# Latent attention: two float16 value parts in place of three bfloat16, and the next batch's norm steps issued earlier

## The chip, the cores and the metric

The kernel runs on one core of a Trainium2 chip. The metric is device time in microseconds, the median of several runs. Within a core TensorE (PE; its weight loads are PEld), VectorE (DVE), ScalarE (ACT) and GpSimd (POOL) each work through their own list of instructions; SyncE (SP) issues DMAs. They meet only at semaphores.

## The reference

A two-layer decoder: causal attention, cross attention and a quantized feed-forward, then an attention with a convolution over its scores, a latent attention and a mixture of experts. The change touches the latent attention alone (`ctx_1024` are 77 context rows per batch, `x` 1024 latent rows per batch; 4 batches, 4 heads of 64):

```python
xn = layernorm(x, ln_x_g, ln_x_b)            # here x is ctx_1024
ln = layernorm(latents, ln_l_g, ln_l_b)      # here the residual stream
q = ln @ W_q
kv = jnp.concatenate([xn @ W_kv, ln @ W_kv], axis=1)
k, v = (kv[..., :INNER], kv[..., INNER:])
q, k, v = (to_heads(q), to_heads(k), to_heads(v))
qn = rmsnorm(q, q_gamma) * SCALE
kn = rmsnorm(k, k_gamma)
sim = jnp.einsum('bhid,bhjd->bhij', qn, kn)
sim = jnp.where(full_mask[:, None, None, :], sim, neg)
attn = jax.nn.softmax(sim.astype(jnp.float32), axis=-1)
out = jnp.einsum('bhij,bhjd->bhid', attn, v)
return out @ W_out + b_out
```

Each query row sees 1024 own keys and 77 context keys.

## The kernel before

`stage_latent_attention` first makes keys and values of the context rows for all batches (the first block), then runs a second block over four batches. A batch has a **preparation** of 14 steps: the normalized rows are transposed, multiplied to queries, keys and values (`multiply_qk`, `multiply_v`), and queries and keys are scaled to unit size. Then comes a **loop of 32 units**. A unit is one head and one tile of 128 query rows; two units make a **pair**, 16 pairs a batch.

The way of a unit: `scores` on TensorE (query halves against the key parts `KH` and `KL`, 1102 columns), then on VectorE `maximum` (mask add, maximum, negation), on ScalarE `exps` and `high` (the float16 upper half), on GpSimd `low` (the float16 lower half, L2936), and from SP one DMA transpose (L2788), which turns both halves. When both units of a pair are turned, `mix_values` multiplies them with the values, ScalarE's `copy_mix` brings the sum to SBUF, `project` multiplies with the output weights, and VectorE's `add` adds to the residual.

The order is written by hand: each engine's block lists its steps for unit u, and `behind(b, u)` those of earlier pairs. On TensorE the mix of pair p comes in unit 2p+5, behind its scores, and the projection in unit 2p+7. The last two mixes of a batch fall into steps 1 and 3 of the next preparation. Score banks come in two, probabilities and halves in three, transposed halves and mix copies in two per pair.

Values are held in three bfloat16 parts of 64 columns: ScalarE copies the product (`value_high`), VectorE subtracts (`value_left`), ScalarE copies the rest (`value_middle`), GpSimd subtracts again (`values_low`). `mix_values` multiplies parts one and two together (128 columns wide, L2864 and L2866), and part three by itself (64 wide, L2870 and L2873, the two probability halves in different column halves of the array).

The next batch's norm runs within the loop: `stats` and `aggregate` on VectorE in units 8 to 14, seven small steps on GpSimd in units 15 to 21 (`rstd_step`; two of them are powers, L2949 and L2959), `apply` on VectorE in units 22 to 29 (L3140), and GpSimd's `add_bias` (L2932) in units 23 to 30.

## Time and profile before

| what | value |
|---|---|
| median of 3 runs | 3918.76 us (3916.62 to 3923.54) |
| profiled execution | 3912.23 us, span 3910.5 us |
| PE, share of the span | 86% |
| DVE | 75% |
| ACT | 67% |
| POOL | 47% |
| DMA queue q1, share of 16 engines | 60.7% |

The shares are means over stages with different limits. The latent attention runs from about 2678 to 3361 us of the span, so a change in it is read from rows of that stretch. A row of the timeline gives start, duration, engine, line, operation, what it writes and reads, and in brackets the idle time of the engine before it and what ended that.

### The profile page before, as it was taken

How to read it: one execution, taken by the hardware profiler on the slowest of the kernel's cores; microseconds unless marked ns; L12 is line 12 of the kernel's file. 1: busy time of each engine (PE TensorE's matmuls, PEld its weight loads, DVE VectorE, ACT ScalarE, POOL GpSimd, SP SyncE). 2: the span in 40 equal slices, each digit the busy share in tenths (PEclk: the TensorE clock that was granted, in tenths of full speed). 3: DMA queues.
4: the chain of work that ended last, by engine and by line, in shares of the span. 5: the costliest groups of instructions: out<-in, count | busy, mean ns of one | idle time of the engine just before them, and what ended most of it. 6: DMA issues, size and time to landing. Idle time of an engine off the chain costs nothing. (4 is left out here: it accounts for less than half of the span.)

```text
span 3910.5 us, 61085 instructions
## 1 busy us (share of the span) xinstructions
PE 3369.3 (86%) x20113; PEld 2602.9 (67%) x20113; DVE 2928.5 (75%) x5833; ACT 2601.1 (67%) x3897; POOL 1826.9 (47%) x1129
## 2 busy tenths in 40 slices
PE   6867724269999999999999999995889899799999
PEld 4645521147777777777777777773667667699999
DVE  4568789779888888888888889984676666474347
ACT  2334444558888888898888989982667667354443
POOL 0034410016656566565665656642767576360015
PEclk9989956589999999999999999997999999799999
DMA  1047800038889888888888889891749467743224
GB/s 51 0 87 129 147 22 1 1 110 157 151 147 154 147 151 151 146 156 143 154 146 151 155 149 162 162 165 36 124 85 174 80 121 140 204 149 95 76 83 146
DMA packets 1571351, 470.02 MB, mean 120 GB/s; under 512 B 1507174, under 2 KB 1565159, under 8 KB 1569767
## 3 DMA queue, kind: packets, MB, share of 16 engines
q1 hardware_dynamic: 1564903, 449.40, 60.7%
q0 software_dynamic: 6144, 16.79, 1.3%
q8 instruction: 164, 2.69, 0.3%
q14 instruction: 140, 1.15, 0.1%
HBM read 49.00 MB, written 39.58 MB: 23 GB/s over the span
## 5 line engine op out<-in xcount | busy, mean ns | idle before, releaser
L2331 DVE TENSOR_REDUCE d_neg_max<-psum 128x1 f32<-128x1024 f32 x512 | 624.6, 1220 | 161.9 <-PE psum L2066 160.7
L2066 PE MATMUL psum<-d_KH,d_QH 128*128 128x512 f32 x2048 | 685.3, 416 | 25.5 <-DVE d_halves L2340 21.0
L2222 ACT ACTIVATE psum<-psum,d_bias 128x1024 f32<-128x1024 f32 x512 | 558.2, 1090 | 213.9 <-DVE d_bias L2335 203.5
L2340 DVE SCALAR_TENSOR_TENSOR d_halves<-psum,d_halves 128x1024 f16<-128x1024 f32 x512 | 624.3, 1219 | 32.3 <-ACT d_halves L2229 27.7
L2066 PE MATMUL psum<-d_KL,d_QH 128*128 128x512 f32 x2048 | 638.1, 393 | 0.0
L2066 PE MATMUL psum<-d_KH,d_QL 128*128 128x512 f32 x2048 | 636.7, 392 | 0.0
L2022 POOL TENSOR_TENSOR d_KC<-d_KC,d_tap_of 128x1024 f32<-128x1024 f32 x126 | 302.1, 2397 | 536.6 <-ACT d_tap_of L2211 536.6
L2229 ACT ACTIVATE d_halves<-psum 128x1024 f16<-128x1024 f32 x512 | 521.6, 1019 | 3.5
L2066 PEld LDWEIGHTS psum<-d_KH,d_QH 128*128 128x128 f32 x2048 | 356.9, 188 | 173.1 <-issue 68.4
L2066 PEld LDWEIGHTS psum<-d_KL,d_QH 128*128 128x128 f32 x2048 | 384.9, 188 | 87.7
L2066 PEld LDWEIGHTS psum<-d_KH,d_QL 128*128 128x128 f32 x2048 | 384.9, 188 | 87.0
L2029 POOL TENSOR_TENSOR d_KL<-d_KC,d_KH 128x1024 fp32r<-128x1024 f32 x128 | 308.1, 2407 | 112.7 <-ACT d_KH L2217 112.7
L2936 POOL TENSOR_TENSOR e_halves<-e_probs,e_halves 128x1102 f16<-128x1102 f32 x128 | 292.2, 2283 | 122.9 <-ACT e_halves L3037 121.5
L2018 POOL TENSOR_TENSOR d_KC<-d_KC,d_tap_of 128x1024 f32<-128x1024 f32 x126 | 306.8, 2435 | 26.2 <-ACT d_tap_of L2211 17.9
L2211 ACT ACTIVATE d_tap_of<-d_K,d_taps 128x1024 f32<-128x1024 f32 x252 | 288.8, 1146 | 0.0
L3030 ACT ACTIVATE e_probs<-psum,e_neg_max 128x1102 f32<-128x1102 f32 x128 | 150.3, 1174 | 92.9 <-DVE e_neg_max L3109 92.8
L3105 DVE TENSOR_REDUCE e_own_neg_max<-psum 128x1 f32<-128x1102 f32 x128 | 167.1, 1305 | 4.4
L3494 POOL DMA_INDIRECT f_tile<-f_expert_out,f_slots x64 | 60.8, 950 | 231.7 <-DMA f_expert_out<-f_tile 183.8
L3781 DVE TENSOR_TENSOR f_hT_low<-psum,f_hT_high 128x384 fp32r<-128x384 f32 x135 | 75.3, 558 | 117.4 <-ACT f_hT_high L3657 117.2
L3653 ACT ACTIVATE f_silu<-psum 128x352 f32<-128x352 f32 x135 | 62.8, 466 | 145.7 <-PE psum L3543 143.0
L3037 ACT ACTIVATE e_halves<-e_probs 128x1102 f16<-128x1102 f32 x128 | 143.7, 1122 | 23.6 <-DMA e_probsT<-e_halves 20.4
L3657 ACT ACTIVATE f_hT_high<-psum 128x384 fp32r<-128x384 f32 x135 | 66.4, 492 | 137.1 <-PE psum L3563 137.0
(526 smaller groups left out, 7577.7 us busy)
## 6 DMA issues: line engine op xcount, KB each, us to landing
f_weights_raw<-in_L_ffn_packed_dram SPq DMA_DIRECT2D x10, 1088.0 KB, 16.1
f_tile<-expert_rows SPq DMA_DIRECT2D x71, 128.0 KB, 2.2
f_expert_out<-f_tile SPq DMA_DIRECT2D x71, 128.0 KB, 1.7
d_probsT<-d_halves SPq DMA_TRANSPOSE x512, 4.3
f_tile<-f_kept_rows SPq DMA_DIRECT2D x64, 128.0 KB, 2.2
expert_rows<-d_group_mixT SPq DMA_DIRECT2D x7, 1024.0 KB, 11.5
residual_stream<-in_x_dram SPq DMA_DIRECT2D x4, 1024.0 KB, 9.5
f_kept_rows<-residual_stream SPq DMA_DIRECT2D x4, 1024.0 KB, 8.5
```

The costliest lines, as they stand in the source:

```text
L2018: g.tensor_tensor(KC[:, ch, :], KC[:, ch, :], tap_of[:, ch, :], ALU.add)\
L2022: g.tensor_tensor(KC[:, ch, :], KC[:, ch, :], tap_of[:, ch, :], ALU.add)\
L2029: g.tensor_tensor(KL[hh % 2][:, ch, :], KC[:, ch, :], KH[hh % 2][:, ch, :].bitcast(F32), ALU.subtract).then_inc(key_low.sem, 1)
L2066: last = t.matmul(scores_at(u)[:, cols], q_part[:, ch, j * P:(j + 1) * P], k_part[hh % 2][:, ch, cols], start=k == 0, stop=k == 5)
L2211: a.activation(tap_of[:, ch, :], K[b % 2][:, ch, k:S + k], ACT.Copy, scale=taps[:, ch, 3 * h + k:3 * h + k + 1]).then_inc(tapped.sem, 1)
L2222: a.activation(scores_at(u), scores_at(u), ACT.Exp, bias=bias[u % 2][:, 0:1], accum_out=sums[u // 4 % 4][:, u % 4, :]).then_inc(probs_read ...
L2229: a.activation(halves[u % 4][:, 0, :], scores_at(u), ACT.Copy, scale=LIFT)\
L2331: v.tensor_reduce(neg_max[u % 2][:], scores_at(u), AXIS.X, ALU.max, negate=True)\
L2340: v.scalar_tensor_tensor(halves[u % 4][:, 1, :], scores_at(u), LIFT, halves[u % 4][:, 0, :], ALU.mult, ALU.subtract).then_inc(probs_low.se ...
L2936: g.tensor_tensor(halves[i % 3][:, 1, 0:W], probs[i % 3][:], halves[i % 3][:, 0, 0:W], ALU.subtract)\
L3030: a.activation(probs[g % 3][:], scores_at(g), ACT.Exp, bias=neg_max[g % 2][:, 0:1], accum_out=sums[p % 2][:, i:i + 1]).then_inc(probs_read ...
L3105: v.tensor_reduce(own_neg_max[g % 2][:], scores_at(u), AXIS.X, ALU.max, negate=True)\
```

## The change

Values: two float16 parts in place of three bfloat16. So that float16 can hold them, they are multiplied by a power of two, `v_scale`, which bounds them by the norm of the gains, shifts and value weights; it is worked out before the loops by three squares with sums on ScalarE, a product with ones on TensorE, a power on GpSimd and some operations of one column on VectorE. The output weights `wo` are multiplied by the inverse once, on ScalarE in unit 3 of the first batch. `value_middle`, `values_low` and the products of the third part are gone; `value_low` on VectorE multiplies and subtracts in one operation.

Norm steps: `stats` and `aggregate` start in unit 3 in place of 8, `rstd_step` in 9 in place of 15, `add_bias` in 22 in place of 23; `apply` stays in units 22 to 29. `apply` becomes a scalar_tensor_tensor with the reciprocal spread over 256 columns as second tensor.

```diff
@@ mix_values (TensorE)
-                    if p == 0:
-                        t.wait_ge(v_low.sem, v_low.at(TB * (b + 1)))
...
                     for k in range(TB):
                         for part in range(2):
-                            t.matmul(mix_bank, V[:, k, h, 0:2 * HD], moving(part, k), start=k + part == 0, stop=False)
+                            t.matmul(mix_bank, V[:, k, h, :], moving(part, k), start=k + part == 0, stop=False)
                     for part in range(2):
-                        t.matmul(mix_bank, ctx_values[:, b, h, 0:2 * HD], moving(part, TB)[0:Z, :], start=False,
-                                 stop=False)
-                    for k in range(TB):
-                        for part in range(2):
-                            t.matmul(mix_bank[part * HD:(part + 1) * HD, :], V[:, k, h, 2 * HD:3 * HD],
-                                     moving(part, k), start=False, stop=False)
-                    for part in range(2):
-                        last = t.matmul(mix_bank[part * HD:(part + 1) * HD, :], ctx_values[:, b, h, 2 * HD:3 * HD],
-                                        moving(part, TB)[0:Z, :], start=False, stop=True)
+                        last = t.matmul(mix_bank, ctx_values[:, b, h, :], moving(part, TB)[0:Z, :], start=False,
+                                        stop=part == 1)
@@ before the loops (VectorE, GpSimd, TensorE, ScalarE)
+                    v.tensor_scalar(v_size[:, 0:1], PS[:, 6 * BANK:6 * BANK + 1], float(2 * D), None, ALU.mult)
...
+                    g.wait_ge(v_scaled.sem, v_scaled.at(3))
+                    g.tensor_tensor(v_size[:, 1:2], v_size[:, 0:1], core.minus_half[:, 0:1], ALU.pow)\
+                        .then_inc(v_scaled.sem, 1)
                     norm_pool(g, n, 0, True)
...
+                    t.matmul(PS[:, 6 * BANK:6 * BANK + 3], core.ones[:], v_squares[:], start=True, stop=True)\
+                        .then_inc(v_totalled.sem, 1)
...
+                    a.activation(n.xT[:, 1, 0:DC * D], wv[:].rearrange("p c n -> p (c n)"), ACT.Square,
+                                 accum_out=v_squares[:, 2:3]).then_inc(v_squares_done.sem, 1)
@@ values (ScalarE, VectorE)
-                def value_middle(b, j):
-                    a.wait_ge(v_left.sem, v_left.at(TB * b + j + 1))
-                    a.activation(V[:, j, :, HD:2 * HD], left[j % 2][:], ACT.Copy).then_inc(v_middle.sem, 1)
...
+                def value_low(b, j):
                     v.wait_ge(v_high.sem, v_high.at(TB * b + j + 1))
-                    v.wait_ge(v_low.sem, v_low.at(TB * b + j - 1))
-                    v.tensor_tensor(left[j % 2][:], bank(j % 2)[:, 0:D].rearrange("p (h e) -> p h e", h=H),
-                                    V[:, j, :, 0:HD], ALU.subtract).then_inc(v_left.sem, 1)
+                    v.scalar_tensor_tensor(V[:, j, :, HD:2 * HD],
+                                           bank(j % 2)[:, 0:D].rearrange("p (h e) -> p h e", h=H), v_scale[:, 0:1],
+                                           V[:, j, :, 0:HD], ALU.mult, ALU.subtract).then_inc(v_low.sem, 1)
@@ units (ScalarE)
+                        if b == 0 and u == 3:
+                            a.activation(wo[:], wo[:], ACT.Copy, scale=wo_scale[:, 0:1]).then_inc(wo_scaled.sem, 1)
@@ norm steps (GpSimd, VectorE)
-                        if b + 1 < B and 15 <= u < 22:
-                            rstd_step(b + 1, u - 15)
-                        if b + 1 < B and 23 <= u < 23 + TB:
-                            add_bias(TB * (b + 1) + u - 23)
+                        if b + 1 < B and 9 <= u < 16:
+                            rstd_step(b + 1, u - 9)
+                        if b + 1 < B and 22 <= u < 22 + TB:
+                            add_bias(TB * (b + 1) + u - 22)
...
-                    v.tensor_scalar(n.xn[:, tile, :], X[:, TB * b + tile, :], n.mv[:, tile, 0:1],
-                                    n.rstd[:, tile:tile + 1], ALU.subtract, ALU.mult).then_inc(n.normed.sem, 1)
+                    v.scalar_tensor_tensor(n.xn[:, tile, :], X[:, TB * b + tile, :], n.mv[:, tile, 0:1],
+                                           n.rstd[:, tile:tile + 1].to_broadcast([P, D]), ALU.subtract, ALU.mult)\
+                        .then_inc(n.normed.sem, 1)
...
-                        if b + 1 < B and 8 <= u < 12:
-                            stats(b + 1, 2 * u - 16)
-                            stats(b + 1, 2 * u - 15)
+                        if b + 1 < B and 3 <= u < 7:
+                            stats(b + 1, 2 * u - 6)
+                            stats(b + 1, 2 * u - 5)
```

TensorE, an odd unit of the first batch's loop, in the kernel before: the projection of one pair, the mix of another, then the next unit's first scores.

```order
L2882 MATMUL psum<-e_wo,e_mixT 128x256 x2
L2864 MATMUL psum<-e_probsT,e_V 128x256 x16
L2866 MATMUL psum<-e_probsT,e_ctx_values 128x256 x2
L2870 MATMUL psum<-e_probsT,e_V 64x256 x16
L2873 MATMUL psum<-e_probsT,e_ctx_values 64x256 x2
L2845 MATMUL psum<-e_KH,e_QS 128x512
```

The same place now:

```order
L2917 MATMUL psum<-e_wo,e_mixT 128x256 x2
L2905 MATMUL psum<-e_probsT,e_V 128x256 x16
L2907 MATMUL psum<-e_probsT,e_ctx_values 128x256 x2
L2888 MATMUL psum<-e_KH,e_QS 128x512
L2889 MATMUL psum<-e_KL,e_QS 128x512
```

The 18 products of 64 columns are gone, and nothing else of the row has moved.

GpSimd, the end of the norm steps in the first batch's loop, in the kernel before (`e_ln_rstd` is the reciprocal that `apply` reads, the `residual_stream` rows are bias adds):

```order
673 L2959 TENSOR_TENSOR e_ln_tmp<-e_ln_tmp,minus_half 128x8
674 L2936 TENSOR_TENSOR e_halves<-e_probs_33320,e_halves 128x1102
675 L2962 TENSOR_TENSOR e_ln_rstd<-e_ln_tmp 128x8
676 L2936 TENSOR_TENSOR e_halves<-e_probs_33321,e_halves 128x1102
677 L2936 TENSOR_TENSOR e_halves<-e_probs_33322,e_halves 128x1102
678 L2932 TENSOR_TENSOR residual_stream<-residual_stream,e_bo 128x256
```

The same steps now:

```order
667 L2989 TENSOR_TENSOR e_ln_tmp<-e_ln_tmp,minus_half 128x8
668 L2966 TENSOR_TENSOR e_halves<-e_probs_33341,e_halves 128x1102
669 L2992 TENSOR_TENSOR e_ln_rstd<-e_ln_tmp 128x8
670 L2966 TENSOR_TENSOR e_halves<-e_probs_33342,e_halves 128x1102
671 L2966 TENSOR_TENSOR e_halves<-e_probs_33343,e_halves 128x1102
672 L2966 TENSOR_TENSOR e_halves<-e_probs_33341,e_halves 128x1102
673 L2966 TENSOR_TENSOR e_halves<-e_probs_33342,e_halves 128x1102
674 L2966 TENSOR_TENSOR e_halves<-e_probs_33343,e_halves 128x1102
675 L2966 TENSOR_TENSOR e_halves<-e_probs_33341,e_halves 128x1102
676 L2966 TENSOR_TENSOR e_halves<-e_probs_33342,e_halves 128x1102
677 L2962 TENSOR_TENSOR residual_stream<-residual_stream,e_bo 128x256
```

Between the reciprocal and the first bias add stand seven subtractions of a unit where there were two; the order of the steps is the same.

## Rows read from the trace of the kernel before

**Rows 1.** Busy by stretch: us, PE, PEld, DVE, ACT, POOL, PEclk, DMA share, GB/s.
```profile
2757.00:2867.00 110.00, 101.05 (x748) 80.86 (x747) 76.89 (x162) 78.85 (x110) 80.45 (x47) 0.94 0.92 160
...
2875.00:2906.00 31.00, 26.82 (x150) 16.62 (x147) 22.05 (x32) 16.46 (x30) 19.01 (x15) 1.00 0.00 1
...
3089.00:3098.00 9.00, 7.19 (x29) 5.31 (x28) 4.19 (x9) 6.76 (x10) 6.84 (x4) 0.52 1.12 209
```

**Rows 2.** Timeline, TensorE, one mix of the last batch and the scores behind it.
```profile
3281.15 1.91 PE L2864 MATMUL psum<-e_probsT,e_V 128*128 128x256 f16 x16
...
3283.21 1.06 PE L2870 MATMUL psum<-e_probsT,e_V 128*64 128x256 f16 x16
...
3284.32 0.50 PE L2845 MATMUL psum<-e_KH,e_QS 128*128 128x512 f32 x1
```

**Rows 3.** Timeline, TensorE, second and fourteenth mix of the second and last batch.
```profile
2940.81 1.91 PE L2864 MATMUL psum<-e_probsT,e_V 128*128 128x256 f16 x16
...
3021.78 1.91 PE L2864 MATMUL psum<-e_probsT,e_V 128*128 128x256 f16 x16
...
3261.85 1.91 PE L2864 MATMUL psum<-e_probsT,e_V 128*128 128x256 f16 x16
...
3341.21 1.91 PE L2864 MATMUL psum<-e_probsT,e_V 128*128 128x256 f16 x16
```

**Rows 4.** Timeline, the way of one pair in the last batch.
```profile
3277.89 0.50 PE L2845 MATMUL psum<-e_KH,e_QS 128*128 128x512 f32 x1
...
3281.05 0.23 DVE L3102 TENSOR_TENSOR psum<-psum,e_lowered 128x78 f32<-128x78 f32 x1
3281.08 1.18 ACT L3030 ACTIVATE e_probs<-psum,e_neg_max 128x1102 f32<-128x1102 f32 x1 [1.43 <-DVE e_neg_max L3109]
...
3282.38 1.12 ACT L3037 ACTIVATE e_halves<-e_probs 128x1102 f16<-128x1102 f32 x1
...
3283.41 1.16 ACT L3030 ACTIVATE e_probs<-psum,e_neg_max 128x1102 f32<-128x1102 f32 x1
3283.58 2.29 POOL L2936 TENSOR_TENSOR e_halves<-e_probs,e_halves 128x1102 f16<-128x1102 f32 x1 [1.84 <-ACT e_halves L3037]
...
3286.03 1.12 ACT L3037 ACTIVATE e_halves<-e_probs 128x1102 f16<-128x1102 f32 x1 [1.36 <-DMA e_probsT<-e_halves]
```

**Rows 5.** The transposes over the stage: issue on SP in ns, landing.
```profile
L2788 SPq DMA_TRANSPOSE e_probsT<-e_halves x128: 2636/2768/3834, 2764.8 to 3348.7; - x128
...
DMA to landing us min/median/max: 4.5/4.8/6.8
```

**Rows 6.** By line, ns min/median/max: apply, unit, floor; reciprocal waited for; powers.
```profile
L3140 DVE TENSOR_SCALAR e_ln_xn<-residual_stream,e_ln_mean_var,e_ln_rstd x24: 406/946/2032, 2836.8 to 3180.8; 128x256 f32<-128x256 f32 x24
...
  POOL e_ln_rstd L2962: 4.9, 3
...
L3074 DVE TENSOR_TENSOR e_unit<-e_raw,e_inv x32: 1214/1218/1745, 2722.1 to 3228.2; 128x1024 f32<-128x1024 f32 x32
...
L2918 POOL TENSOR_SCALAR e_floor<-e_size x32: 251/1152/1286, 2720.0 to 3225.0; 128x8 f32<-128x8 f32 x32
...
L2949 POOL TENSOR_TENSOR e_ln_tmp<-e_ln_tmp,minus_half 128x8 f32<-128x8 f32 x3 | 4.9, 1640 | 0.0
```

**Rows 7.** Timeline, the second batch's preparation, behind mix 14.
```profile
2876.40 3.70 PE L2808 MATMUL psum<-e_wqk,e_ln_xT 128*128 128x512 f32 x8
...
2878.43 0.60 ACT L2994 ACTIVATE e_raw<-psum 128x512 f32<-128x512 f32 x1 [4.53 <-PE psum L2808]
```

**Rows 8.** Timeline, the end of the second batch's preparation.
```profile
2911.85 0.72 ACT L3017 ACTIVATE e_V<-e_v_left 128x256 bf16<-128x256 f32 x2
...
2913.75 0.42 DVE L3096 TENSOR_TENSOR e_v_left<-psum,e_V 128x256 f32<-128x256 f32 x1 [0.20 <-POOL e_V L2927]
```

**Rows 9.** Timeline, before the loops.
```profile
2683.79 1.01 POOL L2677 TENSOR_TENSOR e_pre_rstd<-e_pre_var_eps,minus_half 77x4 f32<-77x4 f32 x1
...
2698.82 1.06 ACT L2723 ACTIVATE e_ctx_values<-e_pre_left 77x1024 bf16<-77x1024 f32 x1 [1.44 <-DVE e_pre_raw L2641]
```

115 lines of the change are left out of this document (70 added, 45 removed).

## The prediction

> **What bounds the kernel now.** I read the views in this order: the busy time by stretch, to find what stops in the stage that the change touches; the timeline of one pair of units, to see which engine sets the pace; the rows of the transposing DMA; then the waits around the norm steps. The stage runs four times through a loop of 32 units (16 pairs), with a preparation of some 50 us between two loops. In a loop TensorE is busy 101.05 of 110.00 us, and the DMA engines show a share of 0.92 [rows 1]: two candidates. The timeline says which one it is. In the last batch the scores of one pair start at 3277.89 and those of the next at 3284.32 [rows 2, 4]: 6.43 us, and TensorE works through them without a gap. So a quiet pair is bound by TensorE at 6.44. Over twelve pairs (second mix to fourteenth) the second batch takes 3021.78 - 2940.81 = 80.97 and the last, which has no norm steps, 3341.21 - 3261.85 = 79.36 [rows 3], or 6.75 and 6.61 per pair. What is over 6.44 comes from late transposes and from the norm steps.
>
> **Part 1, the third product is gone.** The 64-wide products of the third value part and their two context products run from 3283.21 to 3284.32 [rows 2]: 1.11 us per pair, so TensorE alone would go at 6.43 - 1.11 = 5.32. Full gain would be 64 x 1.11 = 71 us. It isn't reached, because another loop is next late. Mix(p) stands behind the scores of unit 2p+5 and waits for both transposes of its pair. Counted from the start of the pair's first scores (3277.89): the second unit's mask add starts at 3.16, its exponential at 5.52 [rows 4]. ScalarE's conversion follows an exponential by 3282.38 - 3281.08 = 1.30, GpSimd's subtraction that by 3283.58 - 3282.38 = 1.20 [rows 4], and it takes 2.28. That puts the second transpose at 10.3. The first unit's subtraction ends at 7.97, so its transpose holds the SP queue to 8.05 + 2.77 = 10.8 [rows 5], and the second lands at 10.9 + 4.7 = 15.6 (4.7 lies between the least and the median landing). On TensorE the mix's place comes two periods after the pair's own scores, plus the scores and the projection ahead of it, 3281.15 - 3277.89 = 3.26 [rows 2, 4]. With TensorE idle for the difference: 2C + 3.26 + (C - 5.32) = 15.6, so C = 5.9. Today 2 x 6.44 + 3.26 = 16.1 leaves 0.6 of slack, which is why a quiet pair doesn't wait.
>
> Late transposes come on top: landing takes 4.5 to 6.8 us, 4.8 in the median [rows 5], and one late by 1.4 stops ScalarE for 1.36 [rows 4]. Today they cost 6.61 - 6.44 = 0.17 per pair against a slack of 0.6. Without slack I take twice that, less for neighbours that have slack of their own: 0.3. So C = 6.2 without norm steps. Bounds: 5.66 (two SP issues of 2.77 and their gaps, no late landing) and 6.6 (each late landing counts fully and the pace stays what it is).
>
> **Part 2, norm steps.** bn_stats, bn_aggr and GpSimd's seven steps move from units 8 to 21 to units 3 to 15. Of these only the two powers of 1.64 matter on GpSimd [rows 6], which has 2.28 of work per unit of 3.1; they are only moved, and now meet a loop without slack: 0.05 per pair, 6.25. What goes is VectorE's wait for the reciprocal at unit 22: 4.9 us in three times [rows 6]. It now has six units of lead; the loop takes a part of that as its gain, already in 6.25. GpSimd's bias adds move one unit up, behind apply operations that VectorE issues before GpSimd's own subtraction of that unit: no wait. SP's queue gets nothing.
>
> The apply itself takes 0.41 alone but 0.95 in the median and up to 2.03 [rows 6], since GpSimd's subtraction runs beside it. It becomes a scalar_tensor_tensor of the residual and a spread reciprocal, two tensors in SBUF. The nearest row for two such inputs is the unit step: 1.21 alone and up to 1.75 beside GpSimd, and GpSimd's floor step of 0.25 takes 1.15 in the median beside it [rows 6]. So the new form is still locked out, and it locks GpSimd out. I leave the four apply pairs of a batch between 6.25 and the 6.65 they show now: 6.5.
>
> The Trainium skill, page "SBUF — State Buffer", section "Who interferes with whom", says that a VectorE instruction with two SBUF inputs contends with a GpSimd instruction that reads SBUF, and that the second to issue blocks fully. By that rule the new form brings nothing over the old one; the rows on the unit step agree (0.25 against 1.15). If the lock did go, the twelve apply pairs would run at 6.25, and the sum would be 3 us better.
>
> **Sum of the loops.** A batch with norm steps: 8 x 6.25 + 4 x 6.5 = 76.0 against 80.97 (I take the second batch for all three), 5.0 each; the last: 12 x 6.2 = 74.4 against 79.36, 5.0. Together 19.9. The first period of each batch starts with an empty pipeline, so its 1.11 counts: 4.4. Loops: 24.3.
>
> **Part 3, between the loops.** The last two mixes of a batch lie in the next preparation. The product of tile 1 starts at 2876.40 behind mix 14, and ScalarE has waited 4.53 for it [rows 7]; mix 15 stands in the same way before tile 3. So 2 x 1.11 x 3 = 6.7. At the very end the mix before the last is covered by the wait for the last transpose, and one counts: 1.1. Together 7.8 (bounds 3 and 9: the chain through GpSimd's inverse runs beside it).
> The value chain loses ScalarE's middle copies (0.72 for two) and GpSimd's third part, for which VectorE waited 0.20 [rows 8]. At the end of the preparation two pairs of middle copies stand before the next high copy; less what is hidden: 1.3 x 4 = 5.2 (bounds 1 and 8).
>
> **Part 4, added work.** Before the loops: two tiny squares and one of 512 columns on ScalarE (idle there until its first operation), a product of three columns, seven tiny VectorE operations, and one power on GpSimd, 1.01 by the nearest row [rows 9]. That power stands ahead of the norm's and pushes the first apply: 0.8 (bounds 0 and 2). The scaling of the output weights, 1024 columns on ScalarE, is 1.06 by the nearest row [rows 9] and stands before the exponential of unit 3 once: 1.1 (bounds 0 and 1.1). The scale on the value copies costs nothing, being an operand of the same operation; the key copies carry one too. Context values lose a copy and a subtraction behind other work: 0. Cost: 1.9.
>
> **Sum:** 24.3 + 7.8 + 5.2 - 1.9 = 35.4. The profiled execution took 3912.23 (span 3910.5), the median is 3918.76, 6.5 above it with all runs between 3916.62 and 3923.54; I subtract from the median: **3883.4**.
>
> **Rivals.**
> A. The pace reaches 5.8 to 5.9, because late landings are absorbed (two of three chains in flight are untouched by one late landing) and apply follows. For it: the queue keeps up with 2.8 per unit where a loop starts, at 209 GB/s against 160 in the loop [rows 1]. Against: the slack is gone. Loops save 3 x (80.97 - 71) + (79.36 - 70) + 4.4 = 44; total 55: 3864. Chance 0.19.
> B. The transposes are the bound already. For it: a DMA share of 0.92 over the loop [rows 1]. Against: 1.12 at the faster start of a loop, so 0.92 is not full. Then the loops give 4.4 and perhaps 2, the rest 11: 3902. Chance 0.14.
> C. Slower: TensorE now idles some 0.9 us in each pair, and the granted clock falls to half. Place: the mix's wait. Price: at 0.52 [rows 1] the 5.3 us of work in a pair become 10.6, which is 4.4 over the pace of 6.2; eight such pairs of the 64 use up the gain of 35.4; with twelve the time is 3883.4 + 12 x 4.4 = 3936. Against: in the preparation TensorE was busy 26.82 of 31.00 us, 0.87, at a granted clock of 1.00 [rows 1], and the new loop has 5.3 of 6.2, 0.86. Chance 0.03.
> D. The forecast, 3872 to 3895: 0.64. That the spread form doesn't free VectorE is part of it (3 us either way, and the rule of the skill is weighed there).
>
> **How the numbers follow.** Range: A's lower end is C = 5.7 throughout, 3855; B's upper end is 3906. Between 3858 and 3904 lie D, most of A and most of B. Within 0.2% means 3911 to 3927, about what a measurement of this kernel can tell from no change; only B with costs at their bounds gets there: 0.03. Slower 0.03, faster 0.94.
>
> **What would show it.** Right: twelve pairs in 74 to 77 us; TensorE waiting for a transpose before many mixes, where now a quiet pair has no gap; VectorE's wait for the reciprocal gone; the new apply still between 0.4 and 2 us; preparation 3 to 4 us shorter. Rival A shows as pairs under 6.0, B as pairs of 6.6 with TensorE waiting over 1 us in each, C as a granted clock under 1.00 within the loops. The prediction is wrong if the apply pairs run as quickly as the others, or if something that isn't in the chain (ScalarE's order of exponential, copy and mix copy) becomes the pace.

## The result and the profile after

| kernel | median | runs | ratio to before (95% interval) |
|---|---|---|---|
| before | 3923.54 us | 5, 3916.62 to 3927.74 | |
| changed | 3892.76 us | 5, 3889.41 to 3901.38 | 0.993 (0.9912 to 0.9947) |

Faster by 30.8 us. The forecast was 35.4 less and 3883.4: 9.4 us too low and within its range. Of these, 4.8 are the median of before, which two more runs put at 3923.54; the gain itself is 4.6 short. The profiled execution of the changed kernel is its slowest, 3901.38 us with a span of 3899.6, only 10.9 below the span of before. Most of what is missing there lies outside the latent attention: the same code took 8.5 us more ahead of the stage and 5.4 more behind it. The stage itself went from 682.8 to 658.0 us, 24.8 less; the sums below are made against this. How far one execution can be trusted is told by the kernel with the old form of apply (below), whose time is the same within the intervals and whose stage took 651.3. One of the twelve runs of the values alone (below) took 4099.03 us at a granted clock of 0.81, the others 0.93, and its ratio leaves this run out.

Busy time by stretch, of the changed kernel: the first batch's loop as in [rows 1], a stretch of the last batch's loop, and the start of the fourth preparation (us, then busy us of PE, PEld, DVE, ACT, POOL, then granted clock, DMA share, GB/s).

```profile
2757.00:2867.00 110.00, 91.05 (x515) 73.94 (x516) 83.62 (x170) 79.98 (x114) 79.50 (x47) 0.92 0.85 152
3240.00:3350.00 110.00, 86.62 (x508) 68.90 (x508) 58.33 (x124) 68.58 (x98) 65.14 (x29) 0.92 0.93 161
...
3173.00:3187.00 14.00, 10.42 (x46) 6.60 (x45) 2.15 (x6) 6.78 (x11) 6.47 (x4) 0.76 0.73 128
```

TensorE is busy 91.05 of 110 us where it was 101.05, with a third fewer instructions. Its slack is real; the loop is not shorter by as much. The rows that answer to [rows 3], timeline of TensorE, second and fourteenth mix of the second and of the last batch:

```profile
2941.24 1.91 PE L2905 MATMUL psum<-e_probsT,e_V 128*128 128x256 f16 x16
...
3017.34 1.91 PE L2905 MATMUL psum<-e_probsT,e_V 128*128 128x256 f16 x16
...
3248.05 1.91 PE L2905 MATMUL psum<-e_probsT,e_V 128*128 128x256 f16 x16
...
3327.02 1.91 PE L2905 MATMUL psum<-e_probsT,e_V 128*128 128x256 f16 x16
```

Twelve pairs of the second batch take 76.1 us (80.97 before), those of the last 78.97 (79.36 before). So the batches with norm steps gained, and the last one, which has none, gained nothing. The waits over the stage tell what stands in the way (engine, line, what it waited for: us in total, times, longest):

```profile
ACT e_probs L3053 <- DVE e_neg_max L3131: 60.8, 50, 3.8
ACT e_halves L3060 <- DMA e_probsT<-e_halves: 43.0, 41, 2.6
...
PE psum L2905 <- issue: 14.6, 22, 2.3
```

ScalarE's conversion (L3060) waits for a transpose to give a buffer of halves back: 43.0 us, where the kernel before had this in 20.4 us:

```profile
ACT e_halves L3037 <- DMA e_probsT<-e_halves: 20.4, 27, 1.6
```

"issue" ahead of the mix (L2905) is TensorE standing at the wait for two transposes: 26 of the 64 mixes begin 0.09 us after the second transpose of their pair has landed, where the kernel before had 11 such mixes. The rows on the transposes over the stage, which answer to [rows 5], haven't moved:

```profile
L2831 SPq DMA_TRANSPOSE e_probsT<-e_halves x128: 2592/2752/3786, 2776.2 to 3335.4; - x128
...
DMA to landing us min/median/max: 4.5/4.8/6.7
```

One such stop in the last batch, timeline of ScalarE and TensorE (in brackets the idle time ahead and what ended it):

```profile
3278.70 1.12 ACT L3060 ACTIVATE e_halves<-e_probs 128x1102 f16<-128x1102 f32 x1 [2.61 <-DMA e_probsT<-e_halves]
...
3279.73 0.37 ACT L3045 ACTIVATE e_mixT<-psum 128x256 f32<-128x256 f32 x1
...
3280.15 2.07 PE L2917 MATMUL psum<-e_wo,e_mixT 128*128 128x256 f32 x4 [2.46 <-ACT e_mixT L3045]
...
3282.01 2.48 PE L2905 MATMUL psum<-e_probsT,e_V 128*128 128x256 f16 x16
```

A transpose is late, the conversion waits 2.61, and the mix copy stands behind the conversion on ScalarE; so the projection waits 2.46. Behind this stop the granted clock falls to half (0.76 in the mean over 3277 to 3284), and the projection takes 2.07 where it took 1.13. This pair took 8.7 us.

Where the stage's time went, from the starts in both timelines (us; the four numbers are the batches):

| part | before | after | difference |
|---|---|---|---|
| up to the first batch's transposes of normalized rows | 33.2 | 34.8 | +1.6 |
| first preparation | 45.5 | 46.7 | +1.2 |
| first scores to second mix | 24.3, 24.0, 23.8, 24.7 | 23.3, 23.0, 23.3, 23.3 | -3.9 |
| twelve pairs | 82.8, 81.0, 81.0, 79.4 | 76.7, 76.1, 76.6, 79.0 | -15.7 |
| fourteenth mix to next preparation | 3.2 three times | 2.0 three times | -3.6 |
| preparations two to four | 49.9, 53.8, 50.5 | 48.2, 51.8, 51.8 | -2.4 |
| from the last fourteenth mix to the end | 19.7 | 17.7 | -2.1 |

### The profile page after: what moved, and what is told of

It reads as the page before. It is cut to its first block and busy times, and to the rows that moved or that the text cites. A ratio compares the mean times of both kernels' runs of the same rounds, so it can differ in the third digit from the quotient of the medians.

```text
span 3899.6 us, 58697 instructions
## 1 busy us (share of the span) xinstructions
PE 3319.5 (85%) x18960; PEld 2562.3 (66%) x18963; DVE 2929.8 (75%) x5839; ACT 2593.3 (67%) x3871; POOL 1806.3 (46%) x1098
## 3 DMA queue, kind: packets, MB, share of 16 engines
q14 instruction: 139, 1.14, 0.1%
## 5 line engine op out<-in xcount | busy, mean ns | idle before, releaser
L2029 POOL TENSOR_TENSOR d_KL<-d_KC,d_KH 128x1024 fp32r<-128x1024 f32 x128 | 308.2, 2408 | 112.7 <-ACT d_KH L2217 112.7
L3060 ACT ACTIVATE e_halves<-e_probs 128x1102 f16<-128x1102 f32 x128 | 143.6, 1122 | 46.0 <-DMA e_probsT<-e_halves 43.0
```

The source lines that it names most:

```text
L2029: g.tensor_tensor(KL[hh % 2][:, ch, :], KC[:, ch, :], KH[hh % 2][:, ch, :].bitcast(F32), ALU.subtract).then_inc(key_low.sem, 1)
```

## The experiments

All ran on a chip together with the kernel before, whose medians beside them were 3921.7 us (values alone, norm steps alone, old apply, later mix), 3923.4 (stats moved, upper halves alone, no low keys, both doors) and 3926.9 (the other four). So a median can differ by 5 us from one of another group without a cause; the ratios are free of that. My theory after the result: the third product's time on TensorE became a loop bound by the transposes, and the norm steps that moved matter little. The rival: the two halves of the change need each other.

### Values alone, and norm steps alone

The first takes the changed kernel and puts the norm steps back; the second takes the kernel before and moves them.

```diff
@@ values alone: norm steps as before (GpSimd; stats, aggregates and apply likewise)
...
-                        if b + 1 < B and 9 <= u < 16:
-                            rstd_step(b + 1, u - 9)
+                        if b + 1 < B and 15 <= u < 22:
+                            rstd_step(b + 1, u - 15)
...
```

> The changed kernel with the norm steps back in their old units and the apply in its old form, so the two float16 value parts alone. My theory (the gain is the third product's 1.11 us per pair, cut short by the way from scores to landed transpose): nearly the whole gain stays, some 27 of 31 us, 3896; twelve pairs 77 to 79 us in a batch with norm steps, 74 to 79 in the last; VectorE waits again some 5 us in three times for the reciprocal. Rival (the norm steps carry the gain in the first three batches): under 15 us gained, twelve pairs over 79.

> The kernel before with the norm steps moved and the new form of the apply; values stay in three bfloat16 parts. My theory: 2 to 5 us under the kernel before, since only the wait for the reciprocal (4.9 us over three batches) goes; twelve pairs 79 to 80.5 in place of 81 to 83. Rival (norm steps carry the gain): 15 us or more.

Values alone: 3910.52 us, ratio 0.9964 (0.9951 to 0.9978). Norm steps alone: 3921.91, ratio 0.9997 (0.9984 to 1.0011). Apart they give some 11 and 0 us, together 31, or 25 with the old form of apply, which ran beside them (below). So 14 to 20 us, half the gain or more, are an interaction. My expectation for the values alone was 14 too low, and of the 2 to 5 us that I expected of the norm steps alone the median shows none (their twelve pairs in the three norm batches, 81.9, 80.6 and 80.0, are 2.3 shorter in sum). The twelve pairs of the three norm batches, values alone, took 79.9, 81.1 and 79.2, nearly what they took before.

### The old form of apply

```diff
-                    v.scalar_tensor_tensor(n.xn[:, tile, :], X[:, TB * b + tile, :], n.mv[:, tile, 0:1],
-                                           n.rstd[:, tile:tile + 1].to_broadcast([P, D]), ALU.subtract, ALU.mult)\
+                    v.tensor_scalar(n.xn[:, tile, :], X[:, TB * b + tile, :], n.mv[:, tile, 0:1],
+                                    n.rstd[:, tile:tile + 1], ALU.subtract, ALU.mult).then_inc(n.normed.sem, 1)
```

> The changed kernel with tensor_scalar for the apply, and all else kept. If both forms are locked out by GpSimd alike (my theory): the same time within 3 us, the apply at 0.9 to 1.0 us in the median. If the spread form avoids GpSimd: 5 us or more slower, the four apply pairs of a batch 0.3 us longer each.

3896.86 us, ratio 0.9929 (0.991 to 0.9949); 4 above the changed kernel with overlapping intervals. The spread reciprocal brings nothing that can be told from none (what it does to single pairs is told with the last experiment). Therefore the interaction is in where the steps stand.

### Which of the moved steps counts

Only VectorE's stats and aggregates in their new units, GpSimd's steps and the bias adds in their old ones, and apply in its old form:

> The changed kernel with its values and with VectorE's stats and aggregates in units 3 to 9, but with GpSimd's seven steps back in units 15 to 21, the bias adds back in unit 23 and the old form of apply. Values alone gave 3910.5, the changed kernel with the old form of apply 3896.9. If it is VectorE's wait for the reciprocal at unit 22 (5.7 us in three times in the values-only kernel) that costs those 14 us, nothing is gained here: 3908 to 3912, and the wait stays. If it is the stats on VectorE, which in units 8 to 14 meet a loop without slack and in units 3 to 9 one that is still filling, the time is that of the full change: 3893 to 3899, whatever the wait for the reciprocal does.

3906.93 us, ratio 0.9948 (0.9935 to 0.9962): 1 us below what the wait predicts, far from 3893 to 3899. VectorE's wait for the reciprocal over the stage, then the timeline of the first batch around unit 22:

```profile
DVE e_ln_xn L3162 <- POOL e_ln_rstd L2992: 9.4, 3, 3.3
```

```profile
2841.21 1.12 ACT L3060 ACTIVATE e_halves<-e_probs 128x1102 f16<-128x1102 f32 x1 [2.35 <-DMA e_probsT<-e_halves]
...
2842.41 2.28 POOL L2966 TENSOR_TENSOR e_halves<-e_probs,e_halves 128x1102 f16<-128x1102 f32 x1 [0.74 <-ACT e_halves L3060]
...
2844.65 0.20 POOL L2992 TENSOR_TENSOR e_ln_rstd<-e_ln_tmp 128x8 f32<-128x8 f32 x1
...
2844.95 2.48 DVE L3162 TENSOR_SCALAR e_ln_xn<-residual_stream,e_ln_mean_var,e_ln_rstd 128x256 f32<-128x256 f32 x1 [3.28 <-POOL e_ln_rstd L2992]
...
2849.16 1.18 ACT L3053 ACTIVATE e_probs<-psum,e_neg_max 128x1102 f32<-128x1102 f32 x1 [4.23 <-DVE e_neg_max L3131]
```

Read it downwards. A transpose is late, so the conversion is, so GpSimd's subtraction is, and the last reciprocal step stands behind that subtraction. VectorE waits 3.28 us for it, and its apply then takes 2.48 beside the next subtraction. The maximum of unit 23, whose scores were ready, stands behind the apply on VectorE, and ScalarE waits 4.23 for it. The pair takes 10.15 us, and 11.67 and 10.85 in the next two batches. That the third product would have covered some of this is argued, not shown: the kernel before with slack for its transposes (below) has stops of some 5 us at this place as well.

The other test starts from values alone and moves VectorE's apply two units later, with GpSimd's bias adds behind it in unit 24; all else keeps its old place:

```diff
...
-                        if b + 1 < B and 22 <= u < 22 + TB:
-                            apply(b + 1, u - 22)
+                        if b + 1 < B and 24 <= u < 24 + TB:
+                            apply(b + 1, u - 24)
```

> The values-only kernel (3910.5) with VectorE's apply and GpSimd's bias adds in units 24 to 31 in place of 22 and 23; stats and GpSimd's seven steps stay where they were before. Theory: what the moved norm steps bring once the third product is gone is the wait for the reciprocal, since VectorE's apply stands ahead of the next maximum (in the run with only the stats moved VectorE waited 3.28 us there, then 2.48 us in apply, and ScalarE 4.23 us for the maximum). Two units of lead end that as well as five: no wait for the reciprocal, no pair over 8.5 us in units 20 to 25, and 3893 to 3899. Rival: the place of the stats or of GpSimd's powers (now before the loop is full) is what counts: 3905 to 3912. Apply up to the last unit may cost the next preparation 0 to 1 us each time.

3898.32 us, ratio 0.9922 (0.9903 to 0.9941) where values alone had 0.9964 (0.9951 to 0.9978): 12 us by the medians. The reciprocal isn't waited for any more; the twelve pairs of the norm batches took 79.4, 77.5 and 77.7. What returned is TensorE's wait for the last apply at the start of a preparation, as the waits on that line say:

```profile
L3162 DVE TENSOR_SCALAR e_ln_xn<-residual_stream,e_ln_mean_var,e_ln_rstd x24: 402/1175/2170, 2841.6 to 3173.9; 128x256 f32<-128x256 f32 x24
...
  PE psum L2842: 4.3, 3
```

Both point the same way: most of what the moved steps bring is the lead of the reciprocal over apply, not the place of the stats. The traces say how far. From the first scores to the next preparation the three norm batches together took 316.3 us with values alone, 319.8 with the stats moved, 308.2 with the later apply, and 304.0 in the changed kernel with the old apply: 8 of 12 us. For the rest the new place of the powers isn't excluded, and the whole stage of the later apply (661.7 us, 665.2 with values alone) is only 3.4 shorter in the traced executions.

### What bounds the loop now

Upper halves alone are transposed (the mix multiplies the upper half twice, so TensorE does the same work and the low halves are left out):

```diff
-                    sp.dma_start_transpose(probsT[p % 2][:, :, i, :], halves[g % 3][:].rearrange("p a s -> p (a s)"))\
+                    sp.dma_start_transpose(probsT[p % 2][:, 0:KB, i, :], halves[g % 3][:, 0, :])\
...
-                        return probsT[pair % 2][:, part * KB + k, :, :].rearrange("p i q -> p (i q)")
+                        return probsT[pair % 2][:, k, :, :].rearrange("p i q -> p (i q)")
```

> The changed kernel whose transposing DMA turns the upper halves alone (the mix multiplies the upper half twice, so TensorE's work is the same, and the output is not the reference's). Theory: late transposes set the pace of the loops. With half the bytes, landing falls to about 3 us and TensorE's own 5.3 to 5.4 per pair is next: twelve pairs in 64 to 67 us where the changed kernel has 76 to 79, 3835 to 3850 in all. Rival: the transposes are not what is late, and a ring through ScalarE and VectorE (exponential, copies, maximum) or TensorE at half clock sets the pace: pairs stay at 6.2 or more, over 3880.

3862.18 us, ratio 0.984 (0.9825 to 0.9855), 31 below the changed kernel, though 12 above the upper end of what the theory gave, for a reason that its norm batches show (below). Its transposes, and TensorE in the last batch's loop (columns as in the first fence):

```profile
L2831 SPq DMA_TRANSPOSE e_probsT<-e_halves x128: 1272/1292/2154, 2776.4 to 3301.0; - x128
...
DMA to landing us min/median/max: 3.2/3.2/5.1
```

```profile
3222.00:3305.00 83.00, 76.31 (x491) 63.41 (x489) 58.58 (x124) 68.44 (x99) 65.48 (x29) 1.00 0.63 107
```

The last batch's twelve pairs fell from 78.97 to 66.96, or 5.58 each, with single pairs at 5.13 (3277.75 to 3282.88 on the timeline), through which TensorE works without a gap: that is its own pace, and the granted clock stays at 1.00. In the norm batches quiet pairs did the same, but the four pairs with apply stood at 6.78 one after the other. So the transposes bound the changed kernel's quiet pairs, and behind them lies another bound for the apply pairs; the last experiment shows which.

The opposite relief, an eighth of TensorE's busy time taken away (the products with the low key parts are left out):

```diff
-                        t.matmul(scores_at(u)[:, cols], query, KH[:, h, cols], start=True, stop=False)
-                        t.matmul(scores_at(u)[:, cols], query, KL[:, h, cols], start=False, stop=True)
+                        t.matmul(scores_at(u)[:, cols], query, KH[:, h, cols], start=True, stop=True)
```

> The changed kernel whose scores leave out the products with the low key parts of the own rows (the output is not the reference's): 4 products of 512 columns less per pair, about 0.9 us of TensorE. Theory: TensorE has slack in every pair now, so only the first periods of a batch and the stretches at half clock gain: 5 to 12 us, 3881 to 3888. Rival: TensorE's work is still on the ring that sets the pace (scores, exponential, halves, transposes, mix, mix copy, projection): a good part of 64 x 0.9 = 58 comes, below 3860. Third: with still less to do TensorE's clock is halved more often, and nothing or less comes: over 3890.

3893.88 us, ratio 0.9925 (0.9909 to 0.994): no gain, against the 5 to 12 that I expected. TensorE in the first batch's loop, in the last batch from the first scores to the end, and in a part of it at full clock; then the last batch of the changed kernel:

```profile
2757.00:2867.00 110.00, 79.60 (x482) 64.04 (x480) 84.22 (x173) 84.66 (x121) 81.66 (x47) 0.91 0.89 161
...
3221.00:3337.00 116.00, 85.94 (x480) 66.86 (x480) 68.39 (x145) 78.72 (x112) 72.94 (x32) 0.85 0.92 164
...
3275.00:3294.00 19.00, 14.24 (x94) 11.29 (x93) 14.62 (x32) 15.86 (x23) 13.50 (x7) 1.00 1.03 191
```

```profile
3225.00:3345.00 120.00, 95.63 (x544) 75.90 (x543) 68.65 (x144) 79.09 (x112) 73.11 (x32) 0.91 0.91 158
```

79.60 us of work in 110 where there were 91.05, and the norm loops only some 1 us shorter (100.4, 99.3 and 101.6 from first scores to the next preparation), the last twelve pairs 2. The third expectation (over 3890, since the clock falls more often) fits the time, and the clock did fall: 0.90, 0.90, 0.85 and 0.85 over the four batches, where the changed kernel has 0.93, 0.93, 0.92 and 0.91. So this run alone can't tell a TensorE off the path from one that lost by its clock what it gained in work. The stretch at full clock can: its three pairs take 6.30, 6.52 and 5.65, with TensorE idle for a quarter of it. In the loop TensorE is off the path, except through its clock.

### Two doors for a late transpose

A late transpose reaches the loop at the mix (TensorE) and at the conversion that needs its halves back (ScalarE). Each is given slack alone, then both. First every mix two units later, with three buffers of transposed halves:

```diff
@@ the mix; its copy, the projection, the add and the third buffer likewise
...
-                    if u >= 5 and u % 2 and (u - 5) // 2 < PAIRS:
-                        mix_values(b, (u - 5) // 2)
...
+                    if u >= 7 and u % 2 and (u - 7) // 2 < PAIRS:
+                        mix_values(b, (u - 7) // 2)
...
```

> The changed kernel with the mix, its copy, the projection and the add of a pair each one pair later, and three buffers for turned halves in place of two. It takes the way from scores to landed transpose out of the path without touching any operation. My theory (that way is the bound at C = 5.9): pairs fall to 5.7 to 5.9, twelve pairs 69 to 72 us, some 20 us less, 3872; TensorE's waits for transposes are gone. Rival (the queue or the DMA engines are the bound by their rate, or ScalarE's wait for a free half buffer is): twelve pairs stay at 76, time within 5 us of the changed kernel.

3892.75 us, ratio 0.9927 (0.991 to 0.9945). The last batch fell (first scores to the end: 111.5 us, 119.9 in the changed kernel) and the loops of the norm batches by about 1 each; the preparations, three of which now hold one mix more, grew by 1.5 in the mean. TensorE no longer waits for a transpose (one mix of 64 begins at a landing), but ScalarE does, 48.0 us in 57 times. The medians show no gain, as the rival had it, though the rival's reason fails for the last batch, whose twelve pairs took 72.5 in place of 79.0.

Then four buffers of halves in place of three, and nothing else:

```diff
-                    if g >= 3:
-                        a.wait_ge(turned[(g - 3) % 4].sem, unit_turned(g - 3))
+                    if g >= 4:
+                        a.wait_ge(turned[(g - 4) % 4].sem, unit_turned(g - 4))
...
```

> The changed kernel with four buffers of halves in place of three and nothing else; the mixes stay where they are. Theory: late transposes reach the loop by two doors, the mix (TensorE) and the conversion that needs its halves back (ScalarE). With one door shut the other still holds the pace, as it did with the later mix alone (no gain): 3886 to 3895. Rival: ScalarE's door is the one that counts, since behind it wait the mix copy, the projection and the next mix: near the 3872 of both together, 3870 to 3880.

3891.73 us, ratio 0.991 (0.9892 to 0.9928), against 0.993 (0.9912 to 0.9947): nothing that can be told from none. ScalarE no longer waits for a transpose, and TensorE waits for it instead, 33.6 us in 33 times (14.6 in 22 in the changed kernel), and 37 of its mixes begin at a landing:

```profile
PE psum L2905 <- issue: 33.6, 33, 2.2
```

Both together:

> The changed kernel with every mix two units later (three buffers of transposed halves, as in the earlier run with 3892.75) and with four buffers of halves in place of three, so that ScalarE's conversion waits for the transpose four units back. Theory: what is left of late transposes comes through that wait (43 us in 41 waits in the changed kernel, the longest 2.6). Then the twelve pairs of the last batch fall below the 72 us of the earlier run, to 66 to 69, and the norm batches by as much less what apply holds: 3875 to 3885. Rival: the norm batches are held at 6.78 per pair by apply and the lock with GpSimd, and the rest is given back in the preparations: 3888 to 3895.

3872.26 us (3870.03 to 3882.11), ratio 0.9877 (0.9861 to 0.9892): 3 us below the theory's range, and the best complete kernel of this study, 20.5 us below the changed one. TensorE in the last batch's loop:

```profile
3224.00:3312.00 88.00, 74.49 (x483) 61.68 (x482) 55.80 (x118) 64.38 (x93) 61.05 (x27) 1.00 1.11 194
```

The transposes' engines are at a share of 1.11 and 194 GB/s, where the changed kernel had 0.93 and 161: late landings are absorbed (TensorE waits for one once, 2.6 us; ScalarE still 20.5 in 27 times), and the loop runs near the pace of the transfers. From first scores to the next preparation it takes 95.4, 95.4 and 95.0 us, where the changed kernel takes 102.0, 101.0 and 101.9. The expected 66 to 69 us for the last batch's twelve pairs did not come: 71.7, after 72.5 without the fourth buffer. What fell are the norm batches, and there the pairs with apply stay at 6.78.

Was that slack wanted before the change as well?

> The kernel before with both buffers of slack (mixes two units later, four halves). Theory: before, TensorE bound a quiet pair at 6.44, and late transposes cost 0.17 per pair, so there is at most 64 x 0.17 = 11 us and the wait for the reciprocal to gain: 3908 to 3920. Rival: the transposes bound it before as well, and it gains what the changed kernel gained by the same edit, 20 us: about 3900.

3919.54 us, ratio 0.9983 (0.9972 to 0.9995): 7 us, within the theory's range. Two mixes of its last batch, timeline of TensorE:

```profile
3270.12 1.91 PE L2864 MATMUL psum<-e_probsT,e_V 128*128 128x256 f16 x16
...
3276.56 1.91 PE L2864 MATMUL psum<-e_probsT,e_V 128*128 128x256 f16 x16
```

6.44 apart, and nearly every pair of that batch's loop is at 6.43 to 6.45: there TensorE was the bound of the kernel before, and the transposes were not. But the 7 us are not the price of late transposes before the change. This kernel still has its norm steps in their old places, and VectorE's wait for the reciprocal was 7.2 us in three times (4.9 before):

```profile
DVE e_ln_xn L3140 <- POOL e_ln_rstd L2962: 7.2, 3, 2.4
```

Three pairs, one in each norm batch, took 11.90, 11.20 and 11.52, some 5 us over 6.44 each, and its preparations, which hold one mix more, took 11 us more than before. In the last batch, from the first scores to the end, the slack is worth 5.6 us here (118.2 for 123.8) and 7.4 after the change (112.5 for 119.9). So what sets the two kernels apart lies mostly in the norm batches and between them; with the norm steps moved as well, slack wasn't run on the kernel before.

### Apply on one column

The changed kernel again, with the rows of the later batches left without their norm:

```diff
-                    v.scalar_tensor_tensor(n.xn[:, tile, :], X[:, TB * b + tile, :], n.mv[:, tile, 0:1],
-                                           n.rstd[:, tile:tile + 1].to_broadcast([P, D]), ALU.subtract, ALU.mult)\
+                    v.scalar_tensor_tensor(n.xn[:, tile, 0:1], X[:, TB * b + tile, 0:1], n.mv[:, tile, 0:1],
+                                           n.rstd[:, tile:tile + 1], ALU.subtract, ALU.mult)\
```

> The changed kernel whose apply covers one column in place of 256 (the rows of the later batches are not normalized, so the output is not the reference's); its place, its waits and its count are the same. It prices apply in the loops. Forecast at the prediction: twelve apply pairs fall from 6.5 to 6.25, 3 us: about 3890. Rival by the later runs, where apply pairs stand at 6.78 whatever the transposes do: VectorE, locked out for 1.85 us of GpSimd's 2.28, is the bound in them, and twelve pairs fall by 0.5 each, and with them what waits behind: 6 to 9 us, 3884 to 3887.

3896.44 us, ratio 0.9917 (0.9899 to 0.9935): no gain, and neither expectation held. It didn't take the lock away, as I had thought it would, and this shows the lock better than anything else here. By line (ns min/median/max), then the timeline of VectorE and GpSimd:

```profile
L3162 DVE SCALAR_TENSOR_TENSOR e_ln_xn<-residual_stream,e_ln_mean_var,e_ln_rstd x24: 207/756/1876, 2839.7 to 3164.4; 128x1 f32<-128x1 f32 x24
```

```profile
2852.59 2.28 POOL L2966 TENSOR_TENSOR e_halves<-e_probs,e_halves 128x1102 f16<-128x1102 f32 x1 [0.30 <-ACT e_halves L3060]
...
2853.32 1.57 DVE L3162 SCALAR_TENSOR_TENSOR e_ln_xn<-residual_stream,e_ln_mean_var,e_ln_rstd 128x1 f32<-128x1 f32 x1
```

One column takes 0.21 us alone and here 1.57: it ends at 2854.89, and GpSimd's subtraction at 2854.87. It isn't one instance. 18 of the 24 applies end 0.01 to 0.02 us behind a subtraction that was running when they began; in the old form 18 and 20 end 0.15 behind one (kernel before, old apply), in the spread form 20 of 24 end 0.28 behind (changed kernel). So what apply takes is the rest of GpSimd's instruction and then 0.02, 0.15 or 0.28 of its own.

The same rows name the bound of the apply pairs. VectorE's next maximum stands behind apply, so a ring closes: subtraction, rest of apply, maximum, exponential, conversion, and the subtraction two units on. Timeline of the changed kernel:

```profile
2852.97 2.28 POOL L2966 TENSOR_TENSOR e_halves<-e_probs,e_halves 128x1102 f16<-128x1102 f32 x1 [0.41 <-ACT e_halves L3060]
...
2853.68 1.85 DVE L3162 SCALAR_TENSOR_TENSOR e_ln_xn<-residual_stream,e_ln_mean_var,e_ln_rstd 128x256 f32<-128x256 f32 x1
...
2857.25 1.18 ACT L3053 ACTIVATE e_probs<-psum,e_neg_max 128x1102 f32<-128x1102 f32 x1 [1.14 <-DVE e_neg_max L3131]
...
2858.55 1.12 ACT L3060 ACTIVATE e_halves<-e_probs 128x1102 f16<-128x1102 f32 x1
...
2859.75 2.28 POOL L2966 TENSOR_TENSOR e_halves<-e_probs,e_halves 128x1102 f16<-128x1102 f32 x1 [0.39 <-ACT e_halves L3060]
```

From 2852.97 to 2859.75 are 6.78 us: 2.28 of subtraction, 0.28 of apply behind it, 1.72 to the exponential, 1.30 to the conversion and 1.20 to the next subtraction. TensorE and the transposes have no part in it, so it holds whatever is done to them. It also gives the other forms: 6.50 and 0.15 are 6.65, and the kernels with the old form have 6.64 and 6.65 in the second batch (the kernel before and old apply); 6.50 and 0.02 are 6.52, and this kernel has 6.51, 6.52 and 6.52 there. So apply's size was worth 0.26 per apply pair, and the spread form costs 0.13 over the old one, both too little to be seen in a median.

So what apply costs in a loop is decided by its place against the subtraction, not by its size. The lock as such was not taken away in any run. An estimate of it: where the transposes are halved the last batch has 5.58 per pair and the apply pairs 6.78, which is 14 us for twelve of them; in the changed kernel, with 6.58 per pair in the last batch, it is 2.4. A reciprocal held in PSUM, which would leave one SBUF operand, wasn't tried.

## Why the prediction was nearly right

**What bounds the kernel.** Right: TensorE bound a quiet pair at 6.44 before (the kernel with slack ran 6.44 throughout), and with the product gone the transposes do (halving them took the last batch's twelve pairs from 79.0 to 67.0; taking an eighth of TensorE's work away took them to 76.9). In the apply pairs it is the ring through the lock, at 6.65 before and 6.78 after, which the prediction didn't have. Rival A, which had the late landings absorbed by what slack there is, is out for this kernel: it takes the two added buffers and the later mix to absorb them. Rival B is out in its strong form, since loops with late landings absorbed run faster than 6.2 per pair.

**Part 1, C = 6.2 without norm steps.** The mechanism held and the size was off. The last batch took 78.97, 6.58 per pair, not 74.4. The chain's 5.9 was fair: pairs of 5.9 to 6.2 are frequent between the stops, as from 3248.05 to the next mix at 3254.00. The term that failed is "late transposes come on top: 0.3", worked from a stop of 1.36. Without slack at either door a late landing costs its lateness on ScalarE, then again through the mix copy and the projection, and then TensorE's half clock; the pair shown above is 2.5 us over 6.2. In six kernels with the same last loop (the changed one, values alone, old apply, stats moved, late apply, apply on one column) the twelve pairs took 76.3 to 79.1, 78.3 in the mean or 6.5 per pair: 0.6 for late landings and clock over 5.9, twice what I took. (Two slips change nothing: 16.1 less 15.6 is 0.5 of slack, not 0.6, and 0.25 against 1.15 is GpSimd's floor step, not the unit step.)

Term by term, forecast and measured in the traced stage: twelve pairs 19.9 and 15.7, first periods 4.4 and 3.9, preparations and ends of loops 13.0 and 6.9, start and scaling -1.9 and -1.6 (the measured scaling is in the first periods). That is 35.4 and 24.9 (24.8 unrounded). So the largest shortfall of the traced execution is not the pace of the loops but Part 3.

**Part 2, norm steps.** The number was right and the reason wrong. Forecast 5.0 for each norm batch, measured 6.0, 4.9 and 4.4. I gave the moved steps nothing of their own, as "already in 6.25", and had GpSimd's 4.9 us of waiting gone. The runs show that they carry 14 us (3910.5 for values alone, 3896.9 with them and the old apply). The step that failed is that the wait's price in the new loop would be its price in the old one, 4.9 us in three times. In the loop without the third product it grew to 5.7 and 9.4 (and to 7.2 in the kernel before with slack), with the apply and the maximum behind it some 4 us each. So in each norm batch two errors met: the pace of Part 1 cost some 4 us more than I had (the last batch, to which no norm steps belong, gained 0.4 in place of 5.0), and the moved steps gave some 14/3 = 4.7 that I had put at nothing. That 5.0 came out is luck.
The spread form: right. It is still locked out, at 0.47 to 2.15 us where the old form had 0.41 to 2.03 [rows 6], and exchanging the two is worth nothing. The apply pairs of the changed kernel stood mostly at 6.4 to 6.8, for a forecast of 6.5, and the undisturbed ones at the ring's 6.78. The Trainium skill, page "SBUF — State Buffer", section "Who interferes with whom", which was weighed there, says that a VectorE instruction with two SBUF inputs contends with a GpSimd instruction that reads SBUF, and that the ports they share are an exclusive lock; this case's runs agree, most plainly in the 1.57 us of one column.

**Part 3, between the loops.** Forecast 2.2 of products and 1.3 of values for each passage, measured 1.2 + 1.7, 1.2 + 2.0 and then 1.2 - 1.4, from the two rows of the table. Here 1.2 is the row from the fourteenth mix, the other number the preparation. The fourteenth mix's own 1.2, which I hadn't counted, is mostly given back: from the transposes to the first product are 1.4, 0.3 and 1.5 us more than before, since this product waits for ScalarE, which isn't earlier. Timeline of TensorE, start of the second preparation:

```profile
2875.00 1.98 PE L2851 MATMUL psum<-e_wqk,e_ln_xT 128*128 128x512 f32 x4 [2.97 <-ACT e_ln_xT L3014]
...
2877.69 1.91 PE L2905 MATMUL psum<-e_probsT,e_V 128*128 128x256 f16 x16
...
2879.65 3.60 PE L2851 MATMUL psum<-e_wqk,e_ln_xT 128*128 128x512 f32 x8
```

The second of these products is the one of [rows 7]. From the first to it are now 4.65 us, 5.85 before, so the mix between them gave its 1.2. The fourth preparation grew by 1.4. Its first 14 us had a granted clock of 0.76 (first fence), where before they had 1.00, and that this is the whole cause is argued, not shown:

```profile
3187.00:3201.00 14.00, 11.81 (x71) 7.55 (x70) 2.37 (x5) 7.09 (x12) 5.88 (x6) 1.00 0.60 117
```

The value chain was over-sized. It gave 0.5 us in the second preparation, not 1.3. The claim that the scale costs nothing is wrong: the value copies went up. The lines of ScalarE's copy of the changed kernel, of VectorE's subtraction, and of the copy before (busy, mean ns):

```profile
L3117 DVE SCALAR_TENSOR_TENSOR e_V<-psum,e_v_scale,e_V 128x256 f16<-128x256 f32 x32 | 14.5, 476 | 1.8 <-ACT e_V L3039 1.8
L3039 ACT ACTIVATE e_V<-psum,e_v_scale 128x256 f16<-128x256 f32 x30 | 13.9, 475 | 19.2 <-PE psum L2861 18.7
```

```profile
L3012 ACT ACTIVATE e_V<-psum 128x256 bf16<-128x256 f32 x24 | 8.5, 385 | 6.0 <-PE psum L2818 6.0
```

475 against 385 ns for each copy, and these alternate with the products. The kernel before could have told this. Its copies of 512 columns out of PSUM take 598 ns without a scale and 680 with one, though they differ in the type of the output too:

```profile
L3006 ACT ACTIVATE e_KH<-psum,e_k_gamma 128x512 fp32r<-128x512 f32 x32 | 21.8, 680 | 0.0
...
L2994 ACT ACTIVATE e_raw<-psum 128x512 f32<-128x512 f32 x32 | 19.1, 598 | 43.8 <-PE psum L2808 41.6 <-DVE e_unit L3074 1.3 <-issue 0.5
```

So some 0.08 of the 0.09 goes with the scale; the argument that the key copies carry one too was a reason against "nothing".

**Part 4, added work.** The scaling of the output weights took 1.14 for a forecast of 1.06, the power on GpSimd 0.56 for 1.01. The start grew by 1.6 for a forecast of 0.8, in a stretch whose granted clock was 0.60 where the same 33 us of the stage had 0.66; the first preparation by 1.2 where I had a gain of 1.3. These two are 3.3 of the 10.6 us that the traced stage is short of the 35.4.

**Rival C.** It happened in small, and its price of 4.4 us per pair wasn't measured by itself. The changed kernel has two short stretches at half clock within its last loop, each behind a stop of TensorE of 2.5 and 1.8 us (0.76 over 3277 to 3284 and over 3304 to 3311), and one in its third (near 3165). The kernel before has none there beyond the start of a loop. Behind the last scores of the stage both fall (0.76 over 3331 to 3338, and before over 3350 to 3357). The kernel with both doors open ran its last loop at 1.00 beyond its start. So it is a part of the late landings' price, not a case of its own.

## What to carry to other kernels

When the busiest engine of a loop is relieved, every wait that it had covered has to be priced again at the new pace, and a step with one unit of lead is the first that shows. Slack for a late transfer has to be given at all the places that it holds, each buffer's reader and writer, since one alone only moves the wait. An instruction that is locked out by another engine's costs the rest of that instruction, so making it smaller gained nothing here; a place where the other engine is idle is what to look for, and no run here tried one.

## What was not expected of the hardware

A VectorE operation on 128x1 with two SBUF tensors took 1.57 us and ended within 0.02 us of GpSimd's 2.28 us subtraction; on 128x256 it ended 0.28 behind it, and a tensor_scalar of the same size 0.15. Transposing 128x1152 in float16 took 3.2 us to land and 1.29 us of issue, 128x2304 took 4.8 and 2.75: the issue halves with the size, the landing does not. An eighth of TensorE's busy time in a loop could be left out with no change in time, and the granted clock over the four batches went from 0.91 to 0.93 down to 0.85 to 0.90.
